# The self layer's order, the filling and the first period by other tables in a decoder kernel of 48 attention units

## The reference

```python
x = x + L0_attn(layernorm(x))        # self: layernorm, q/k/v, 16 heads of 16, softmax, out projection
x = x + L0_xattn(layernorm(x), ctx)  # cross: keys and values from 120 rows of context
x = x + L0_ffn(layernorm(x))         # linear layer with int4-simulated weights and a LoRA term
x = x + L1_attn(layernorm(x))        # "sigmoid": rms norm, rotary q and k, sigmoid weights
x = x + L1_xattn(layernorm(x), ctx)  # one-head cross attention
x = x + L1_ffn(layernorm(x))         # two of 64 experts per chunk of 128 rows
```

## Time and profile before

| | us |
|---|---|
| median of three runs | 1092.66 (1091.53 to 1095.04) |
| the profiled execution | 1096.01 |
| its span, first to last instruction | 1094.2 |
| TensorE busy in the span | 1020.1 (93%) |
| mean granted TensorE clock | 0.977 |
| filling and period 0 | to about 91 |
| periods 1 to 15 | about 91 to 410 |

### The profile page before, as it was taken

The page is one execution under the profiler, slowest core; times in us unless marked ns, Lnnn a source line. Parts: engine busy times, 40 slices in busy tenths (PEclk is TensorE's granted clock), DMA queues, the critical chain, the costliest instruction groups (busy, mean ns, idle before and its releaser), DMA issues.

```text
span 1094.2 us, 24132 instructions
## 1 busy us (share of the span) xinstructions
PE 1020.1 (93%) x8386; PEld 799.5 (73%) x8386; DVE 762.7 (70%) x1736; ACT 635.6 (58%) x1150; POOL 583.9 (53%) x924
## 2 busy tenths in 40 slices
PE   5679999999987999999999999999999999999967
PEld 4446777777765777877777768878788776778855
DVE  4378777877875756666667888877687763578862
ACT  2136566657654676666665447667576777665530
POOL 3243445455434545555556898878778741124440
PEclk9689999999998999999999999999999999999988
DMA  6775764844553234565545355666657685025666
GB/s 205 89 102 82 120 99 79 123 62 79 92 82 68 51 84 80 97 118 93 93 81 81 41 79 73 89 83 81 84 74 91 85 105 64 15 76 166 186 181 197
DMA packets 123484, 104.81 MB, mean 96 GB/s; under 512 B 26826, under 2 KB 123099, under 8 KB 123355
## 3 DMA queue, kind: packets, MB, share of 16 engines
q1 hardware_dynamic: 117652, 99.58, 53.9%
q10 hardware_dynamic: 5712, 3.68, 1.4%
HBM read 29.34 MB, written 4.19 MB: 31 GB/s over the span
## 4 chain that ended last, share of the span: by engine, by line
PE 83%; DVE 9%; issue 3%; DMA 2%; ACT 2%; POOL 1%; ACTq 0%; DVEq 0%; SPq 0%; POOLq 0%
PE l_ring L1217 11%; PE l_sT L1132 11%; PE l_o L1152 11%; PE l_copy L1198 9%; PE l_ring L1254 7%; PE l_ring L1167 7%; PE l_ring L1237 4%; PE l_copy L1175 4%; PE l_ring L1874 3%; DVE l_nmax L984 3%; PE l_copy L1152 3%; PE l_ring L1265 2%; PE l_sT L1813 2%; PE l_copy L1245 1%; PE l_o L1846 1%
## 5 line engine op out<-in xcount | busy, mean ns | idle before, releaser
L984 DVE TENSOR_REDUCE l_nmax<-l_ring 128x2 f32<-128x512 f32 (+1 forms) x384 | 250.7, 676 | 104.2 <-PE l_ring L1167 101.4
L763 ACT ACTIVATE l_probs<-l_sT 128x1024 f32<-128x1024 f32 (+1 forms) x256 | 257.8, 1025 | 58.9 <-PE l_sT L1132 45.9
L1132 PE MATMUL l_sT<-qstack,kstack 99*128 99x256 bf16 (+2 forms) x1280 | 187.4, 273 | 0.9 <-ACT l_probs L763 0.5
L1167 PE MATMUL l_ring<-kstack,qstack 96*128 96x256 bf16 (+1 forms) x1024 | 141.5, 247 | 26.7 <-issue 16.3
L1132 PEld LDWEIGHTS l_sT<-qstack,kstack 99*128 99x128 bf16 (+2 forms) x1280 | 125.8, 104 | 25.1 <-issue 2.7
L1167 PEld LDWEIGHTS l_ring<-kstack,qstack 96*128 96x128 bf16 x1024 | 78.1, 98 | 79.2 <-issue 32.0
L1217 PE MATMUL l_ring<-wT,l_zT 128*128 128x256 f32 x512 | 126.8, 386 | 1.7 <-DVE l_attn L1022 0.7
L1152 PE MATMUL l_o<-l_probs,v_heads 128*32 128x256 f32 (+1 forms) x2048 | 127.8, 384 | 0.0
L1198 PE MATMUL l_copy<-l_zT,wT 128*128 128x256 f32 x384 | 104.0, 404 | 4.8 <-ACT l_zT L808 2.8
L1217 PEld LDWEIGHTS l_ring<-wT,l_zT 128*128 128x128 f32 x512 | 92.5, 192 | 14.6 <-issue 2.6
L616 POOL TENSOR_SCALAR factors<-mv 128x2 f32<-128x2 f32 (+1 forms) x77 | 19.4, 253 | 155.8 <-DVE mv L1041 86.4
(11 more groups left out here) (219 smaller groups left out, 1960.5 us busy)
## 6 DMA issues: line engine op xcount, KB each, us to landing
qstack<-l_qpart SPq DMA_DIRECT2D x288, 128.0 KB, 4.2
kstack<-l_kpart SPq DMA_DIRECT2D x192, 128.0 KB, 4.4
kstack<-in_experts SPq DMA_DIRECT2D x36, 256.0 KB, 3.0
kstack<-l_kpart SPq DMA_DIRECT2D x96, 60.0 KB, 3.2
qstack<-in_experts SPq DMA_DIRECT2D x20, 256.0 KB, 3.0
...
```

The source lines that it names most:

```text
L763: act.activation(probs[buffer_of(g)][0:kp, :], sT[g % 2][0:kp, :], ACT.Sigmoid if sig(u) else ACT.Exp, scale=HD ** -0.5).then_inc(p_ok, 1)
L984: dve.tensor_reduce(nmax[u % 2][:, tt, h0:h0 + hb], bank("s", u, i)[:, 0:hb * sk].rearrange("p (h k) -> p h k", h=hb), AX_X, ALU.max, nega ...
L1132: i = pe.matmul(sT[g % 2][0:kp, j * S:(j + 1) * S], kstack[slot_of(u)][0:rows_used, col * width(u) + kt * kp:col * width(u) + (kt + 1) * k ...
L1167: m = pe.matmul(out[:, j * sk:(j + 1) * sk], qstack[slot_of(u)][0:STACK, (h0 + j) * S + tt * P:(h0 + j) * S + (tt + 1) * P], kstack[slot_o ...
```

## The change

Three tables are replaced: the order of the self layer, the filling and the first period. The tables of the cross and sigmoid layers, of the drain and of the tail stay. Every job is still there, with the same instructions and the same data; only where it stands in the lists of the engines is different.

```diff
 ORDERS = {
     "self": """
-        np qa sT0 dq0 s sT1 p0q s qb s s pv2 e0 o1 pv3 e1 p0k s s dq1 ka s kb p1q e2 e3 p2q oT1 sT2 sT3 p1k dk1 dk0 dq2
-        q0 dk2 s va rows vb l2 s lf lo nT qm pv0 p2k o0 pv1 xb s q1 aT s sT4 e4 l1 s s z e5 oT0 sT5 s qA sT6 cl xs w s
-        pa e6 lw xf cx st pb sT7 ws e7 fac s qB""",
+        sT0 p0q qa dq0 s sT1 s qb np s s pv2 e0 pv3 o1 e1 s s ka s kb p0k dk0 p1q oT1 sT2 e2 dq1 p2q dq2 sT3 e3 nT p1k
+        dk1 s p2k dk2 lo l1 l2 va q0 rows vb s pv0 pv1 o0 s aT s s sT4 e4 s z cl e5 oT0 ws qm q1 sT5 s qA sT6 e6 fac xs
+        xb s w pa cx e7 st xf pb s lw lf sT7 qB""",
...
-    "xs:0 wi dq0:0 xs:1 rows:0 z:0 xf:0 bi xf:1 bv rows:1 qa:0 qb:0 ka:0 p0q:0 p0k:0 kb:0 p1q:0 p1k:0 p2q:0 dq1:0 "
+    "xf:0 wi xs:0 rows:0 z:0 bi xs:1 xf:1 qa:0 qb:0 bv p0q:0 dq0:0 ka:0 kb:0 p0k:0 dk0:0 dk1:0 rows:1 z:1 p1q:0 "
...
-    "s:1 s:1 s:1 qa:3 s:1 qb:3 s:1 e:0:0 s:1 s:1 ka:3 e:0:1 p0q:3 sT:0:0 dq0:3 e:0:2 rows:4 p2q:3 p0k:3 e:0:3 "
+    "s:1 s:1 qa:3 s:1 qb:3 s:1 p0q:3 dq0:3 s:1 s:1 s:1 e:0:0 sT:0:0 sT:0:1 s:1 p2q:3 dq2:3 s:1 e:0:1 ka:3 kb:3 s:1 "
```

## The result

| | before | changed |
|---|---|---|
| median | 1092.78 (1091.53 to 1095.04, 4 runs) | 1079.49 (1076.61 to 1081.24, 4 runs) |
| profiled execution | 1096.01, span 1094.2 | 1079.66, span 1077.9 |
| mean granted clock | 0.977 | 0.982 |

The changed kernel takes 0.9874 of the time of the kernel before, 95% interval 0.9847 to 0.9901. Predicted were 1077.7 with a range of 1072 to 1088: the sign, the range and the size hold, and the total is 1.8 us off. The parts of the sum are another matter. They have to be read one by one.

What follows compares the result with a forecast made beforehand. The steady self layer was taken as PE-bound, with gains only where PE stands: 5.5 (filling and first period) + 8.0 (all-reduce) + 1.5 (periods 1 to 15) = 15.0, giving 1077.7 from 1092.66; range 1072.5 to 1088.

Steps and rivals of the forecast that it cites:

- All-reduce: Period 11 to 12: `p2k` ahead of `qm` removes a 10.4 us stall, a new 2.4 wait comes before nT:13; gain 8.0.
- (a): Filling: DVE scales the weights ahead of the first statistics, so z:0 reaches PE at 18.2 instead of 16.98, a loss of 1.2.
- (c): Filling: q:1 projected first and unit 2's rows ahead of statistics, so z:2 starts at 38.4 instead of 43.80, 5.4 ahead.
- (b): Filling: ACT copies z:1 at once, not behind unit 0's second parts; done at 28.9 against 30.18.
- (d): Filling after z:2: DVE's maxima set the pace and some lead is lost; 4.2 left at nT:0, between 3 and 6.
- (e): Filling: nT:0's DMA meets a nearly empty queue and takes 4 to 5 us, ends 3.4 and 8.0.
- (f): First period: pv:0.1 waits 1 to 2 us for e3 behind ACT's `p1q:3 p1k:3`, partly absorbed; start gain taken as 5.5.
- Rival B: Filling and first period: start gives only 2.5, since nT lands late again and ACT holds e3; 1080.7; chance 0.12.
- Periods 1 to 15: Steady self layer: oT0 0.1 earlier in 15 periods, 0 taken for the first maxima's waits; 1.5, ends -2 and +3.
- Rival D: Steady periods: ACT's later `p1k` makes every first maxima wait; 1096.7, slower; chance 0.07 in full, 0.09 as a mixture.
- A: All-reduce: POOL's load waits for the maximum, unit 13's nT stalls 4.2 and the clock drops; 1082; chance 0.12.
- C: Gap at 334.31 isn't POOL's doing, so stays; 7 in all, 1085.7; chance 0.10 shared with A and Rival B together.

Runs made afterwards that it cites:

- experiment 3: Kernel before with only `p2k` moved ahead of `qm`: 1088.12, ratio 0.9958; with `p0q`, `dk0` and `dq2` moved earlier too: 1082.98, ratio 0.9890.
- experiment 5: Changed kernel with its filling reordered: b2_fill_fix 1085.71; `nT:0` directly behind unit 0's maxima 1077.50; that with `l0` later and `qm` earlier 1077.76.
- b2_fill_fix: Changed kernel with unit 2's projections and unit 3's rows put ahead of unit 0's first maxima in the filling: 1085.71, ratio 0.9924 to the kernel before.
- a4_dk0_early: Kernel before with only SP's `dk0` moved from behind `dk1` to behind `p0k`: 1090.88, ratio 0.9980.
- experiment 4: a4_dk0_early against other traces, nT:2 to nT:12: it takes 209.3 us, four with the old order 211.8 to 212.4, eight with the new 208.4 to 210.2.
- experiment 6: Changed kernel with `qm` ahead of `pv0` and its two bias copies moved to the first quantising step of period 12: 1079.02, ratio 0.9879 to the kernel before.
- b1_no_reduce: Kernel before with the all-reduce replaced by a plain POOL copy of each partition's own maximum: 1082.36, ratio 0.9905.

## Why the prediction held, and where its steps failed

**What bounds the kernel** held: 49.35 of 50 us busy in 250 to 300 as before, and both gains at the places where PE stood.

**All-reduce.** Right in mechanism and, within 1 us, in size. The cost of 10.4 measured 9.9 to 10.4. The silent stretches moved with `qm` and kept their lengths within 0.2 us. The new stall before nT:13 was 1.96 where 2.4 had been worked out. Missed was the 0.56 at 316.69: DVE's reduction moved with `qm` too, and it stands between two maxima. Also missed was how much rests on the rest of the lists: experiment 3 shows that `p2k` ahead of `qm`, taken alone, would have won 4.7 to 6.6 (the trace at nT of period 16), since unit 15's stack then comes 3.34 us late. The prediction speaks of the copies' new order only for the steady periods and takes 0 for it.

**Filling.** Steps (a) to (c) went in the right direction, and (b) to 0.3 us (28.65 against 28.9). (c) was too small: z:2 at 34.62, not 38.4, since the projections of unit 1 now ran at 2.4 GHz (8 matmuls in 1.97 against 3.75 in the earlier trace rows), while the 8.5 us of the working were taken from a stretch at half clock. The step that failed is (d), "from there DVE's maxima set the pace": 4.2 left at nT:0, measured 1.3, in other executions of this filling up to 4.0. Until 50 us DVE isn't what set the pace: it was busy 3.28 of the 10 us from 40 on. It stood waiting, first for the stacks, which the copies could not fill faster (experiment 5), and then for TensorE at 1.2 GHz. Only from 50 on (8.41 of 10) does the working of (d) fit. No view of the kernel before was read for the DMA engines; the share of 0.77 in the earlier trace rows was there, and twelve copies a unit times their rate would have given the floor of 38 and 54 us. (e) held within its ends, not within its 4 to 5: nT:0 was issued at 63.55 and the scores started at 69.49, 5.9 at most. (f) is half right: ACT did wait, 3.05 us for POOL's rest of k:3 (at 78.05), but no wait is printed before `pv` at 79.15, so it cost TensorE nothing that shows. From the first scores (3.6 ahead) to period 1 (2.4 ahead) 1.2 us went all the same; the waits that are printed there name DVE (0.66 at 76.44, 0.49 at 85.95). Rival B, "the start gives only 2.5", is what the profiled execution shows (2.4), but neither of B's reasons is: nT wasn't late again, no matmul shows a wait for ACT, and most of the time was lost ahead of nT.

On the Trainium skill's rule (DMA: Bandwidth & Descriptors, Queues, rings and completion order) that each DMA engine takes turns between queues that have work: b2_fill_fix has nT's small copy issued at 58.40 and its scores waiting for it until 70.67. By then SP had issued all 36 copies of three units and `l0`, which at 1.11 us each from 25.14 on would be through at 67.4 (an estimate; with the 2.0 to 2.6 us of experiment 5, 69.4 to 70.0). So the small copy came in when those queued ahead of it on the other queue had, and taking turns didn't let it through; this trace and the 8.0 us of the prediction (73.08 - 64.83 = 8.25 in the earlier trace rows) agree with each other and not with what the prediction drew from the rule. How long one turn is here, no view shows.

**Periods 1 to 15.** The sum of 1.5 was too low by about 2. The step that failed is "I take 0 for it", on the first maxima's waits: 4.5 us fell to 2.4. SP's early `dk0` does outweigh the later `p1k`, and a4_dk0_early shows that this one move carries the growth of the lead (3.1 of 3.6 us between nT:2 and nT:12, the rest being within the scatter of experiment 4). Rival D is refuted by the same rows. The 0.1 per period for the pair of maxima can't be told apart in this.

**Rivals A and C.** A supposed that the load waits for the maximum; experiment 6 refutes it, and no half clock followed the 1.96. C is refuted by b1_no_reduce.

So the total came out to 1.8 us by luck: two misses have opposite signs, 3.1 too much for the start and 2.1 too little for the steady periods. (The ends of the range are rounded: 20 under 1092.66 is 1072.7, and B with C would give 1088.7.)
